# Ids of the first set on every partition, C 2 of unit 0 copied on chip, and B 0 of the last two units by DMA in a recommender kernel

## The reference, cut to what matters

```
e = stack([tbl_f[ids[:, f]] for f in range(24)], axis=1)      # [1024, 24, 16]
X0 = e; Xk = e
for W in (W0, W1, W2):                                         # 64 maps each
    Xk = einsum('bfd,bhd,fho->bod', X0, Xk, W.reshape(24, -1, 64))
    outs.append(Xk.sum(axis=2))
h = concat([outs (3 x 64), dense_ctx (16)])                    # [1024, 208]
h = relu(h @ W_top1 + b_top1); h = relu(h @ W_top2 + b_top2); y = h @ W_top3
```

## Time and profile before

| | us |
|---|---|
| time, median of 3 runs | 378.97 (378.82 to 379.12) |
| profiled execution | 375.68 |
| its span | 373.8 |
| PE busy | 357.3 (96%) |
| DVE busy | 307.9 (82%) |
| ACT busy | 190.6 (51%) |
| POOL busy | 219.6 (59%) |

### The profile page before, as it was taken

The page is one execution under the profiler, slowest core; times in us unless marked ns, Lnnn a source line. Parts: engine busy times, 40 slices in busy tenths (PEclk is TensorE's granted clock), DMA queues, the critical chain, the costliest instruction groups (busy, mean ns, idle before and its releaser), DMA issues.

```text
span 373.8 us, 7196 instructions
## 1 busy us (share of the span) xinstructions
PE 357.3 (96%) x2742; PEld 158.6 (42%) x2742; DVE 307.9 (82%) x309; ACT 190.6 (51%) x358; POOL 219.6 (59%) x332
## 2 busy tenths in 40 slices
PE   5977799999999999999999998999999999999997
PEld 2655322422433345434352453444443444444475
DVE  3994399789898999989798969898999998997600
ACT  2231024254343666655657466847474766545564
POOL 5888888888887878888772888888840000000000
PEclk9999999999999999999999999999999999999999
DMA  6169969969999699998999799979996999540000
GB/s 222 32 132 212 236 119 224 243 129 221 235 221 238 124 229 251 244 184 203 234 235 252 143 254 281 277 154 237 274 264 141 244 277 244 133 140 0 1 4 0
DMA packets 56342, 69.97 MB, mean 187 GB/s; under 512 B 30994, under 2 KB 35730, under 8 KB 56307
## 3 DMA queue, kind: packets, MB, share of 16 engines
q1 hardware_dynamic: 48852, 68.00, 75.8%
q0 software_dynamic: 5376, 1.39, 3.9%
q10 hardware_dynamic: 2080, 0.13, 0.4%
HBM read 49.05 MB, written 1.58 MB: 135 GB/s over the span
## 4 chain that ended last, share of the span: by engine, by line
PE 82%; DMA 7%; DVE 5%; ACT 3%; issue 2%; SPq 1%; ACTq 0%; DVEq 0%
PE ps_x L437 51%; PE ps_b L437 11%; PE ps_tower L437 10%; PE ps_turn L437 7%; DVE Z L413 4%; DMA B_sb<-x_sb 3%; PE ps_turn L503 2%; DMA C<-x_scratch 2%; PE ps_turn L511 1%; DMA x_scratch<-x_rows 1%; DVE Z L403 1%; ACT x_diag L746 1%; DMA small_ids_sb<-small_ids 1%; ACT x_sb L734 0%; ACT x_small L904 0%
## 5 line engine op out<-in xcount | busy, mean ns | idle before, releaser
L413 DVE TENSOR_TENSOR Z<-A,ps_b 128x1024 f32<-128x1024 f32 x192 | 221.1, 1217 | 8.9 <-PE ps_x L437 4.6
L236 POOL DMA_INDIRECT x_rows<-tbl,ids_sb x168 | 179.4, 1068 | 55.6 <-POOL pause_sb L247 30.6
L437 PE MATMUL ps_x<-Z,w_sb 128*64 128x512 f32 x768 | 184.2, 598 | 0.7 <-DVE Z L413 0.5
L437 PEld LDWEIGHTS ps_x<-Z,w_sb 128*64 128x64 f32 x768 | 49.3, 136 | 79.9 <-issue 55.3
L403 DVE TENSOR_TENSOR Z<-A,C 128x1024 f32<-128x1024 f32 x48 | 57.8, 1224 | 27.1 <-PE ps_x L437 8.5
L746 ACT ACTIVATE x_diag<-ps_turn,mask_sb 128x192 f32<-128x192 f32 x128 | 50.6, 605 | 13.8 <-PE ps_turn L511 13.8
L437 PE MATMUL ps_x<-Z,w0s_sb 128*64 128x512 f32 x192 | 45.2, 597 | 2.6 <-DVE Z L403 2.4
L729 ACT COPY ps_b<-B_sb 128x1024 f32<-128x1024 f32 x36 | 36.9, 1025 | 9.8 <-DMA B_sb<-x_sb 4.4
L247 POOL MEMSET pause_sb<- 128x144 f32 x160 | 40.0, 250 | 0.1
L759 ACT COPY G<-ps_turn 128x416 f32<-128x416 f32 x31 | 15.7, 505 | 46.6 <-PE ps_turn L437 45.6
L437 PEld LDWEIGHTS ps_turn<-x_diag,x_rows 128*64 128x64 f32 x496 | 25.2, 137 | 17.7 <-issue 17.7
(11 more groups left out here) (70 smaller groups left out, 193.0 us busy)
## 6 DMA issues: line engine op xcount, KB each, us to landing
A<-x_scratch SPq DMA_DIRECT2D x48, 512.0 KB, 11.1
B_sb<-x_sb SPq DMA_DIRECT2D x72, 256.0 KB, 11.7
C<-x_scratch SPq DMA_DIRECT2D x32, 512.0 KB, 6.8
x_rows<-tbl,ids_sb POOLq DMA_INDIRECT x168
x_quarters<-x_scratch SPq DMA_DIRECT2D x16, 96.0 KB
x_scratch<-x_rows SPq DMA_DIRECT2D x7, 192.0 KB, 4.7
w_sb<-w SPq DMA_DIRECT2D x2, 384.0 KB, 4.7
small_sb<-small_tables SPq DMA_DIRECT2D x1, 640.0 KB, 5.0
```

Of the source, the lines that this page charges most:

```text
L236: pool.indirect_dma_start(out=x0_rows[t % 2][:, f * D:(f + 1) * D], out_offset=None, in_=tables[f], in_offset=bass.IndirectOffsetOnAxis(ap ...
L413: nc.vector.tensor_tensor(Z[s % ZR][:, :], A[u % AS][i][:, :], ps_b[j % 2][:, :], ALU.mult)\
L437: return nc.tensor.matmul(out, lhsT, rhs, start=start, stop=stop)
```

## The change

1. The ids of (tile 0, set 0) are loaded with one DMA to all 128 partitions, issued fifth on SP; DVE casts them in place of PE's spread and ACT's copies. The two other rows are spread as before, and are cast first.
2. The two `load_c2_half` DMAs of unit 0 are gone; ACT runs `copy_c(0)` before `copy_x1(0)`. `copy_c` copies its first half after C 0 alone.
3. For units 14 and 15 (`LB` = 14) PE makes no B 0. SP loads it from `x1_sb` to `B0_sb`, which lies in the space of `small_sb`, with 2 DMAs ahead of those of B 1 to 3, and DVE reads it there.

```diff
+LB = 14
 def made_b(u, j):
-    return NJ * u + j + 1 if u < PB else NJ * PB + u - PB + 1
+    return NJ * u + j + 1 if u < PB else NJ * PB + min(u + 1, LB) - PB
...
+        B0_sb = small_sb.rearrange("p c f d -> p (c f d)")[:, 0:COLS]
...
-            sp.dma_start(small_ids_sb[:, :], small_ids).then_inc(small_ids_in, 16)
+            sp.dma_start(small_ids_sb[0:1, IDS:], small_ids[:, IDS:]).then_inc(small_ids_in, 16)
             sp.dma_start(small_rows_sb[:, :], small_rows).then_inc(small_rows_in, 16)
             sp.dma_start(mask_sb[:, :], mask).then_inc(mask_in, 16)
+            sp.dma_start(small_ids_sb[:, 0:IDS], small_ids[:, 0:IDS].to_broadcast([CR, IDS])).then_inc(first_ids_in, 16)
...
-            def load_c2_half(i):
...
+            def load_b0(u):
+                sp.wait_ge(x1_copied, u + 1)
+                if u > LB:
+                    sp.wait_ge(z_ready, made_x2(u - 1, NI - 1))
+                for q in range(2):
+                    src = x1_sb[u % 2][H * q:H * (q + 1):NJ, :].unsqueeze(1)
+                    sp.dma_start(B0_sb[:, HALF * q:HALF * (q + 1)], src.to_broadcast([HR, FR, HALF])).then_inc(b0_in, 16)
...
                 load_a(0, i)
-                if i != 1:
-                    load_c2_half(i)
...
+                if u > LB:
+                    load_b0(u - 1)
                 if u > PB:
                     for k in range(NJ - 1):
                         load_b(u - 1, k)
...
+            load_b0(UNITS - 1)
             for k in range(NJ - 1):
                 load_b(UNITS - 1, k)
...
-            for m in range(len(MADE)):
-                nc.vector.tensor_copy(small_ids_row[m], small_ids_sb[:, IDS * m:IDS * (m + 1)])\
+            for m in range(1, len(MADE)):
+                nc.vector.tensor_copy(small_ids_row[m], small_ids_sb[0:1, IDS * m:IDS * (m + 1)])\
                     .then_inc(small_ids_ready, 1)
+            dve.wait_ge(first_ids_in, 16)
+            nc.vector.tensor_copy(small_ids_f32[0][0:CR, :], small_ids_sb[:, 0:IDS]).then_inc(small_ids_ready, 1)
...
                 if i == 0:
-                    if u < PB or j == 0:
+                    if u >= LB and j == 0:
+                        dve.wait_ge(b0_in, 32 * (u - LB + 1))
+                    elif u < PB or j == 0:
...
-                nc.vector.tensor_tensor(Z[s % ZR][:, :], A[u % AS][i][:, :], ps_b[j % 2][:, :], ALU.mult)\
+                nc.vector.tensor_tensor(Z[s % ZR][:, :], A[u % AS][i][:, :],
+                                        B0_sb if u >= LB and j == 0 else ps_b[j % 2][:, :], ALU.mult)\
...
-                    if n == max(x1_at(u) + 1, 7) and u + 1 < UNITS:
+                    if n == max(x1_at(u) + 1, 7) and u + 1 < LB:
                         make_b(u + 1, 0)
...
-            spread_ids(0)
             spread_ids(1)
...
             def copy_c(u):
-                for i in range(NI - 1):
-                    act.wait_ge(C_in[u % 2][i], 16 * uses(u))
+                c = C[u % 2]
+                act.wait_ge(C_in[u % 2][0], 16 * uses(u))
                 if u >= 2:
                     act.wait_ge(z_ready, made_x1(u - 2, NI - 1))
+                nc.scalar.copy(c[NI - 1][64:128, :], c[0][0:64, :]).then_inc(c_copied, 1)
+                act.wait_ge(C_in[u % 2][1], 16 * uses(u))
                 nc.scalar.copy(c[NI - 1][0:64, :], c[1][64:128, :]).then_inc(c_copied, 1)
-                nc.scalar.copy(c[NI - 1][64:128, :], c[0][0:64, :]).then_inc(c_copied, 1)
...
-            copy_ids(0)
             copy_ids(1)
...
+            copy_c(0)
             copy_x1(0)
             copy_c(1)
```

More of the change, by code:

```diff
@@ L100, in cin_tower @@
         small_rows_sb = sb("small_rows_sb", [CR, max(chunks)])
-        small_ids_sb = sb("small_ids_sb", [1, IDS * len(MADE)], mybir.dt.int32)
+        small_ids_sb = sb("small_ids_sb", [CR, IDS * len(MADE)], mybir.dt.int32)
         ones_sb = sb("ones_sb", [1, 128])
@@ L154, in cin_tower @@
         small_in = [sem(f"small_in{k}") for k in range(SETS)]
-        small_ids_in = sem("small_ids_in")
+        small_ids_in, first_ids_in = sem("small_ids_in"), sem("first_ids_in")
         gathered = [sem(f"gathered{p}") for p in range(2)]
@@ L162, in cin_tower @@
         C_in = [[sem(f"C_in{e}{i}") for i in range(NI - 1)] for e in range(2)]
-        c2_in = sem("c2_in")
+        b0_in = sem("b0_in")
         b_in = [sem(f"b_in{k}") for k in range(NJ - 1)]
@@ L287, in load_c @@
                 sp.dma_start(C[u % 2][i][:, :], src.to_broadcast([HR, FR, COLS])).then_inc(C_in[u % 2][i], 16)
-            def load_c2_half(i):
-                half = C[0][NI - 1][64:128, :] if i == 0 else C[0][NI - 1][0:64, :]
-                src = rows_of(0, FR * i, FR).rearrange("t f c -> (t f) c").unsqueeze(1)
-                sp.dma_start(half, src.to_broadcast([FR, FR, COLS])).then_inc(c2_in, 16)
+            def load_b0(u):
[5 more added lines that the diff above has]
+                    sp.dma_start(B0_sb[:, HALF * q:HALF * (q + 1)], src.to_broadcast([HR, FR, HALF])).then_inc(b0_in, 16)
             def load_b(u, k):
@@ L364, in _ @@
             dve.wait_ge(small_ids_in, 16)
-            for m in range(len(MADE)):
-                nc.vector.tensor_copy(small_ids_row[m], small_ids_sb[:, IDS * m:IDS * (m + 1)])\
+            for m in range(1, len(MADE)):
+                nc.vector.tensor_copy(small_ids_row[m], small_ids_sb[0:1, IDS * m:IDS * (m + 1)])\
                     .then_inc(small_ids_ready, 1)
+            dve.wait_ge(first_ids_in, 16)
+            nc.vector.tensor_copy(small_ids_f32[0][0:CR, :], small_ids_sb[:, 0:IDS]).then_inc(small_ids_ready, 1)
             dve.wait_ge(small_rows_in, 16)
             def make_ones(m):
-                dve.wait_ge(ids_copied, 2 * (m + 1))
+                if m == 0:
+                    dve.wait_ge(small_ids_ready, SETS + 1 + len(MADE))
+                else:
+                    dve.wait_ge(ids_copied, 2 * m)
                 for c in range(chunks[MADE[m][1]]):
@@ L395, in cross1 @@
                     dve.wait_ge(C_in[u % 2][i], 16 * uses(u))
-                elif u == 0:
-                    dve.wait_ge(c2_in, 32)
                 else:
-                    dve.wait_ge(c_copied, 2 * u)
+                    dve.wait_ge(c_copied, 2 * (u + 1))
                 if s == 0:
@@ L445, in spread_ids @@
             def spread_ids(m):
-                pe.wait_ge(small_ids_ready, SETS + 1 + m + 1)
-                if m >= 2:
-                    pe.wait_ge(ids_copied, 2 * (m - 1))
+                pe.wait_ge(small_ids_ready, SETS + 1 + m)
                 for half in range(2):
@@ L712, in copy_c @@
             def copy_c(u):
-                for i in range(NI - 1):
-                    act.wait_ge(C_in[u % 2][i], 16 * uses(u))
+                c = C[u % 2]
+                act.wait_ge(C_in[u % 2][0], 16 * uses(u))
                 if u >= 2:
                     act.wait_ge(z_ready, made_x1(u - 2, NI - 1))
-                c = C[u % 2]
+                nc.scalar.copy(c[NI - 1][64:128, :], c[0][0:64, :]).then_inc(c_copied, 1)
+                act.wait_ge(C_in[u % 2][1], 16 * uses(u))
                 nc.scalar.copy(c[NI - 1][0:64, :], c[1][64:128, :]).then_inc(c_copied, 1)
-                nc.scalar.copy(c[NI - 1][64:128, :], c[0][0:64, :]).then_inc(c_copied, 1)
             def copy_b(u, k):
@@ L891, in copy_ids @@
                 for half in range(2):
-                    act.wait_ge(ids_spread, 2 * m + half + 1)
+                    act.wait_ge(ids_spread, 2 * (m - 1) + half + 1)
                     nc.scalar.copy(small_ids_f32[m][:, IDS // 2 * half:IDS // 2 * (half + 1)], spread_bank(m, half)[:, :])\
                         .then_inc(ids_copied, 1)
-            copy_ids(0)
             copy_ids(1)
```

## The result

| | before | after | ratio (95%) |
|---|---|---|---|
| first comparison, us | 379.0 (377.41 to 379.31, 6 runs) | 374.01 (370.81 to 376.58, 6) | 0.9885 (0.9847 to 0.9923) |
| second, us | 377.51 (374.74 to 382.36, 30) | 375.25 (371.13 to 379.21, 10) | 0.9932 (0.9897 to 0.9966) |

A forecast was written before the change was run, and what follows sets the result against it. PE and DMA were taken as nearly balanced, with gather-timed stores starting the transfers and PE alone bounding after 228. Savings of 1.06 + 0.0 + 0.15 = 1.2 us gave 377.8 us from the 378.97 median; range 375.2 to 379.0.

The forecast's parts named there:

- The two parts give 4.8 by the end of unit 0: Start of the kernel: loading the ids directly gains 2.8 us and copying C 2 on ScalarE 2.0.
- What is left dies in slot 7: PE has no slack at 187.53 and B 1 lands as before, so the start's gain is worth nothing there.
- the 0.15: Tile 2's store was taken to come 0.15 us earlier through the gathers, the only gain counted from the start.
- The store of tile 2 within 1 us of 82.60: Sign that the forecast is right: SP's store of tile 2 hardly moves although PE's start is earlier.
- the bounds of -2.0 to +2.3: Range for tile 2's store as gathers meet VectorE products differently: 2.0 us earlier to 2.3 later.
- The working on the gathers: Up to tile 2's store, a gather starting within a two-SBUF-tile VectorE product takes up to 1.87 us instead of 0.95.
- The two landings of 2.4 and 7.1 us: Last gathers of tiles 2 and 4, issue to store: a gather's wait depends on loads beside it, not queue length.
- The rival that is slower by gathers: Units 0 to 2 meet more gathers, tile 2's store comes 2.3 us late, PE loses it: 380.2 us; chance 0.11.
- Part 3, 0.0 and 1.06: Slots 13 and 14: of two savings of 1.06 us from dropped B 0 matmuls, the first shrinks to 0.0, the second stands.
- priced at 1.9 in the queue: Unit 14's two added B 0 transfers delay B 1 by 1.9 us, so the x2 copy ends at 323.9, not 322.0.
- the start is kept: Queue and slots 7 and 9 shift with the gathers: 373.0 us if all is kept, 375.4 if half; chance 0.16.

The follow-up runs named there:

- part 2 again: Second measurement of the kernel before with only C 2 of unit 0 copied by ScalarE instead of loaded: 377.75 us, ratio 0.9986 to before.
- part 3 alone: Kernel before with only B 0 of units 14 and 15 loaded by DMA: ratio to before 0.9889 (4 runs), then 0.9986 (10 runs).
- parts 1 and 2 alone: Kernel before with first-set ids on all partitions and C 2 of unit 0 copied by ScalarE, B 0 unchanged: ratios to before 0.9907 and 0.994.
- part 2 alone: Kernel before with only C 2 of unit 0 copied by ScalarE instead of loaded: ratios to before 0.9958 and 0.9986.
- the repeated changed kernel: The changed kernel with all three parts, measured again without further edits: 375.25 us, ratio 0.9932 to before.
- PAUSE = 48: Changed kernel with GpSimd's memset between two gathers cut from 144 to 48 elements: 375.26 us, ratio 0.9968 to before.
- parts 1, 2 again: Second measurement of the kernel before with first-set ids on all partitions and C 2 of unit 0 copied: 375.26 us, ratio 0.994 to before.
- part 1: Kernel before with only the first set's ids loaded to all 128 partitions: 378.07 us, ratio 0.9999 to before.

## Why the prediction was wrong, step by step

**The two parts give 4.8 by the end of unit 0: too large.** PE's one-hots did start at 9.18 (8.1 to 9.2 foreseen), though partly by luck: the ids landed at 7.47 instead of 6.3, and PE waited for VectorE's one-hot, not for the table. ScalarE's copy took C 2 out of the wait: the third product follows the second by 2.0 to 2.4 us in all but one execution that has the copy (part 2 again: 3.6, waiting for A 2), by 3.6 to 5.9 where C 2 is loaded. But the second product starts when C 1 lands, and that was taken to move with the one-hots. It did not: 36.1 to 37.2 where the first part is missing and C 2 is loaded, 35.3 to 38.1 with both parts. In the changed kernel C 1 was issued at 26.87 instead of 30.98 and landed at 37.5. The stretch between belongs to the DMA, and the gain in slot 1 is 1.7 on average (with the uncertainty told above), 0.9 in the profiled pair.

**What is left dies in slot 7: the step that failed.** Two things were built on the profiled execution's waits of 0.28 and 1.22: that PE had no slack there, so that the whole lead dies, and that the transfers' times after the store of tile 2 were fixed. The same program ran with no wait in slot 7 and 9 at all (part 3 alone), and slot 1 to 9 took its floor, 159.28, in five more executions. What the runs show in place of the step: parts 1 and 2 alone are 2.8 us faster by the timings, and the lead of slot 1 (1.7 on average) still stands at slot 9 (1.8) and slot 11 (1.5). Unlike the wall that was assumed, most of these loads wait for products that free their buffers, and so move with PE. The issue behind a tile's store does not move freely, but mostly has room: leads of 2.3 and, with an earlier store, 2.9 passed tile 2, and one of 3.1 with the store at 82.48 was cut to 0.85. Had the 0.15 been the 1.5 to 1.8 that the traces carry, the forecast would have been 2.6 to 2.9, inside the measured interval of the second comparison (1.3 to 3.9).

**The store of tile 2 within 1 us of 82.60: not in the changed kernel.** It stood there at 80.17 and 80.97, and it stood at 80.17 to 83.48 over eleven executions with the old pause, inside the bounds of -2.0 to +2.3 but for two (-2.1, and -2.4 in the profiled one of the changed kernel). The working on the gathers holds: up to this store those that were lengthened cost 2.2 us less in the changed kernel's first trace than in that of before, and the store came 2.4 earlier. That it is chance is seen by part 2 alone, which had the store at 81.18 and 83.48. It mattered in one execution only, the one cut above. The two landings of 2.4 and 7.1 us show only that a gather lands later with loads beside it; no run tells whether the length of the queue counts. The rival that is slower by gathers needed a store after 84.4; none came.

**Part 3, 0.0 and 1.06: second right, first too low.** ScalarE waited 2.41 for B 1 of unit 14 (2 to 3 foreseen), and PE 0.43 behind it. The first saving was 0.57 in the profile, 0.82, 0.87 and 1.06 in three others and -0.4 in the repeated changed kernel, 0.6 on average. The second was 1.06 each time. The transfer was priced at 1.9 in the queue; the copy's end came at 321.5 instead of 323.9, since the turn of slot 13 stood 1.7 earlier, at 302.91, and the loads with it. By timing the part is worth 1.1, by the prediction 1.06, by the traces 1.6; that the first two agree is partly luck, since the timing can't tell 1.1 from 1.6.

**The rival "the start is kept"** had the outcome that was seen (375.4 for half, 373.0 for all), with a chance of 0.16. Its mechanism, a queue that shifts as a whole with the gathers, is not shown; the loads that wait for products are. What spoke for it stood in the text: a part of the stores' lateness is the queue. What spoke against it, a stall of 0.28 us in one execution, was too small to be called a wall: the times of before already spread by more than 1 us, and the profiled one was 3.3 under their median.

## What to carry to other kernels

A wait of some tenths of a microsecond in one profile is no proof of a wall: ask for each late transfer what it waits for, and let the ones that wait for a product move with the product. Test an assumed wall by moving its anchor alone (here the gathers' pause), and look in the trace whether it moved: if it did and the end stays, the anchor was another. When the last stage of a full queue has a little air, use it once and measure again, as the same step done for two more units (2.1 us of matmuls saved) made this kernel 4.3 us slower.

## What the runs showed of the hardware

- The same program (part 3 alone, on two chips) took 65.67 and 68.27 us to slot 1 and 39.93 and 38.44 us for slots 9 and 10; where PE does not wait, its steps are the same to 0.02 us in all traces. What differs are landings of DMA and, near the start, the granted clock (1.00, and 0.83 and 0.74 in 24 to 32). On one chip the times of one kernel spread by 4 to 10 us.
- A store issued 9.5 us earlier behind a full queue let the load that waits for it go 0.6 us earlier, and the next small issue on SP took 9.89 us instead of 2.08.
- Waits cost more than their length: after a gap of 3.01 us in PE's work the granted clock was 0.57 on average over 8 us, and after two of 0.97 and 1.19 it was 0.50 for 2 us. With PAUSE = 48 one gap of 1.97 in slot 11 was enough: four matmuls behind it took 1.91 instead of 1.08, and the clock was 0.50 from 264 to 266. Yet a gap of 1.58 (parts 1, 2 again), one of 1.46 (part 2) and even three of 0.57, 1.17 and 1.04 within 5 us (part 1) left it at 1.00. The rule behind it is not shown here.
- On two of five chips all kernels took 30 to 50 us more, with nothing of the program changed. The cause is not known.
- Not settled: why C 1 of unit 0 took 10.7 us from issue to landing in the changed kernel against 5.1 before, and whether the first part is worth anything without the second.
